# A decoder block with experts on one core: order of the last batch, two banks for late second layers, and one bias product for four tiles

## The chip, the core and the metric

The kernel runs on one core of a Trainium2 chip. TensorE (PE) multiplies, VectorE (DVE), ScalarE (ACT) and GpSimd (POOL) do the rest, and SyncE (SP) issues most of the transfers. Each engine works through its own instructions in order and waits on semaphores for the others. The metric is the device time of one execution in microseconds (us), lower is better.

## The reference

x is 4 batches of 1024 rows of 256 floats. Three blocks are added to it one after another, each of them on a layer norm of x:

```python
x = x + attention(layernorm(x))        # 16 heads of 16, scores / 4 - slope_h * |i - j|, softmax over 1024 keys
x = x + cross(layernorm(x), ctx)       # 77 context rows per batch, one head of 256
x = x + experts(layernorm(x))          # 8 experts, the best 2 per row

def experts(flat_x):                   # 4096 rows
    top_vals, top_idx = top_k(flat_x @ W_router + b_router, 2)
    w = softmax(top_vals)              # 0 for the other six
    for e in range(8):
        h = relu(flat_x @ W1[e] + b1[e])          # 256 -> 1024
        out += (h @ W2[e] + b2[e]) * w[:, e]      # 1024 -> 256
```

In the cross block the scores are `(x Wq + bq) (ctx Wk + bk)`; the kernel multiplies the query and key weights beforehand, so that a tile of rows is multiplied with `ctx_keys` (256 x 77) and the part that depends on the context row alone is the row `ctx_bias` (1 x 77).

## The kernel before

**One written order.** The function `plan` writes a list of steps. Every engine goes through this one list and issues the instructions that are its own, so the list fixes the order on PE, ACT, DVE, POOL and SP. `TAKES` holds a guessed duration for each kind of step; with it the planner keeps a clock of its own for each engine (`p.pe` is PE's), and puts a step off while the step that it reads isn't ready by these clocks (`until`).

**Attention.** 16 groups G of 4 heads, four groups to a batch. A group has 64 units. A unit is a `score` (PE, a 128x512 product for one head, line 1000, and near the diagonal a small second one, line 1003) and an `exp` (ACT, line 1233); after four units comes an `attend` (PE, 8 products, line 1014). The row maxima of the next group are worked out beside it: `max` (PE, line 1040, 1043) and `maxed` (DVE, line 1370). At the end of each half of a group come `av` (ACT), `av_turn` (PE, line 1022) and `on` (DVE).

**Side work.** Between the units the planner puts the steps of the batch whose attention is over (`complete`) and of the batch to come (`prepare`). How many is set by `PACE_DONE` and `PACE_NEXT`, one number per batch of the running attention: three of four units add that number to a share, capped at 12, and a step is issued while the share is above 0 and takes its price off (6 for a turn, 11 for half an `out`, 18 for half a `cross`, 16 for half a `cross_out`, 12 for half of `logits`, 4 for `rank`). `complete(b)` is the output projection (`out`, line 1092), a layer norm, the cross block (`cross`, lines 1104 and 1105; `cross_out`, lines 1123 and 1124), a layer norm, the routing (`logits`, line 1135, to `rows`, DVE line 1547), and 16 scatters of rows with their code, weights and number to the experts' regions in memory (`scatter`, POOL, line 1700), one after about every fourth unit: each waits for the `exp` in front of it in the order. The last batch is done in two halves of 512 rows, `FORE` as soon as the first half of the last group is there, and `AFT` after the attention.

**Experts.** 71 blocks of 128 rows. The table that says which expert and which rows each block takes is made in two parts, blocks 0 to 39 from the rows of three batches (`EARLY` is 40), the others once the last batch is routed. For a block n, SP issues two transfers (`load`): the first layer's weights `w1_now` (1 MB, line 967) and the rows `xi` (130 KB, line 971). For block 0 SP waits first for the table and for all scatters of the three batches. PE turns the rows (`xi_turn`, line 1191, bank 0), multiplies them with the first layer (`up`, two halves of 16 products, line 1203, banks 1 to 4), and with the second (`down`, 16 products, line 1221, the bank `AV_BANK`, number 7). ACT and DVE put bias and relu on the hidden rows (lines 1339 and 1615), DVE weighs the output (`yo`, line 1630), and POOL adds it to the result in memory (`added`, line 1714), each after the one before has landed. In the order, `up` of block n+1 and the turn of block n+2 stand ahead of `down` of block n. The two halves of the last batch are put between these steps one by one, from the first block on (`parts` and `next(work)` in `plan`).

**Banks.** PSUM has 8 banks of 512 floats per partition: 0 to 2 for scores, 3 and 4 for maxima, 5 and 6 (the ring "back") for all side steps, 7 for `attend` and, later, for `down`. A `down` waits until `yo` of the block before it has read bank 7.

Of the kernel before, what the change touches and what calls it, by code (L numbers as in the profile page):

```python
# [24 lines left out]
P = 128  # L25
NB, S, D = 4, 1024, 256
# [42 lines left out]
PACE_DONE = (4.0, 3.6, 3.6, 4.4)  # L69
# [147 lines left out]
def plan():  # L217
# [448 lines left out]
    parts = [done, complete(NB - 1, AFT)]  # L666
    while parts:
        parts = [part for part in parts if next(part, "end") != "end"]
        next(work)
# [17 lines left out]
def build(nc, t):  # L687
    p = plan()
    with ExitStack() as ctx:
# [136 lines left out]
        last_of = lambda tiles: tiles[1] - 1  # L826
        av_before = lambda G, ch: p.upto("av", *((G, 0) if ch else (G - 1, NCH - 1)))
# [11 lines left out]
        def _(e):  # L839
            def position_rows(i):  # L840

                for hh in range(HG):
                    e.dma_start(qa[i][SPECIAL:MAX_ROW, hh, :], qspec_dram).then_inc(sem["q_specials"], 16)

# [6 lines left out]
            for kind, *k in p.steps:  # L851
# [100 lines left out]
                elif kind == "load":  # L952
                    n, = k
                    if n == 0:
                        e.wait_ge(sem["table"], p.upto("table", 0, TABLE_PARTS - 1))
                        e.wait_ge(sem["scattered"], n_scatters(NB - 2))
                    elif n == 2:

                        e.wait_ge(sem["attend"], attend_of(LAST, NCH - 1, NT - 1))
                    elif n == EARLY:  # L960
                        e.wait_ge(sem["table"], p.upto("table", 1, TABLE_PARTS - 1))
                        e.wait_ge(sem["scattered"], n_scatters(NB - 1))
                        e.wait_ge(sem["idle_zeroed"], 16 * (NIDLE + 1 + NE))
                    if n >= NW:
                        e.wait_ge(sem["up"], p.upto("up", n - NW, 1))
                    of = e.value_load(expert_of[0:1, n:n + 1], min_val=0, max_val=NE - 1)
                    e.dma_start(w1_now[n % NW][:, :, :], t["w1"][bass.ds(of, 1)].rearrange("a (c p) f -> p (a c) f", p=P)).then_inc(sem[f"w1_in{n % NW}"], 16)
                    if n >= NX:
                        e.wait_ge(sem["added"], 16 * (n - NX + 1))
                    at = e.value_load(row_of[0:1, n:n + 1], min_val=0, max_val=NROW - P)  # L970
                    e.dma_start(xi[n % NX][:, :], rows_in[bass.ds(at, P), :]).then_inc(sem[f"slots_in{n % NX}"], 16)

        @block.tensor
        def _(e):
# [6 lines left out]
            for kind, *k in p.steps:  # L981
# [114 lines left out]
                elif kind == "cross":  # L1096
# [3 lines left out]
                    bank = side_bank(kind, *k, first=first)  # L1100
                    for q in (2 * part, 2 * part + 1):
                        tt, cols = 4 * four + q, slice(q * CTX, (q + 1) * CTX)
                        for c in range(DC):
                            e.matmul(ps[:, bank, cols], xT[:, c, tt * P:(tt + 1) * P], ctx_keys[:, b, c, :], start=(c == 0), stop=False)
                        m = e.matmul(ps[:, bank, cols], ones_row[:, :], ctx_bias[:, b, :], start=False, stop=True)
# [100 lines left out]
                elif kind == "down":  # L1206
                    n, = k
                    if n == 0:
                        e.wait_ge(sem["av"], p.counts["av"])
                        e.wait_ge(sem["weights_in"], 16 * NWEIGHTS)  # L1210
                    else:
                        e.wait_ge(sem["yo"], n)
# [3 lines left out]
                    for c in range(FC):  # L1216
# [4 lines left out]
                        m = e.matmul(ps[:, AV_BANK, 0:D], hidT[n % 2][:, c, :], w2[:, bass.ds(expert, 1), c, :].rearrange("p a f -> p (a f)"),  # L1221
# [133 lines left out]
        def _(e):  # L1355
# [10 lines left out]
            for kind, *k in p.steps:  # L1366
# [251 lines left out]
                elif kind == "yo":  # L1618
# [11 lines left out]
                    e.scalar_tensor_tensor(out=y[:, :], in0=ps[:, AV_BANK, 0:D], scalar=w[:, :], in1=bw[:, :],  # L1630
# [149 lines left out]
```

## Time and profile before

| | us |
|---|---|
| three runs | 1706.52, 1716.07, 1715.55 (median 1715.55) |
| profiled execution, its own time | 1717.18 |
| its span, first to last instruction | 1715.3 |
| mean granted clock of PE in it | 0.979 |
| PE busy | 1629.1 (95% of the span) |
| DVE, ACT, POOL busy | 1025.0, 788.5, 323.5 |

A busy PE is one with a product under way; products overlap, so the length of one says little, and the distance from one start to the next says what it costs. PEld is PE's weight load. "Idle before" is the time for which the engine stood still ahead of an instruction, with what ended it. The granted clock is a share of full speed: 1.00 is 2.4 GHz, 0.50 is 1.2 GHz. The attention runs until about 1124 us, the experts' blocks from about 1133 us to the end.

### The profile page before, as it was taken

What the parts mean: (1) busy time and instruction counts of PE and PEld (TensorE: products, weight loads), DVE (VectorE), ACT (ScalarE), POOL (GpSimd) and SP (SyncE); (2) the same over time, 40 slices, a digit from 0 to 9 for tenths busy, and PEclk for the clock granted to TensorE, in tenths of its full rate; (3) what the DMA queues carried; (4) which work ended last, traced back from release to release, by engine and by line L of the source; (5) the groups of instructions that cost most, each with busy time, mean ns of one, the idle gap of its engine ahead of it and who ended that gap; (6) DMA issues with size and microseconds to landing.
All of it is one profiled execution on the core that took longest, in us unless ns stands there. A gap on an engine that the chain in (4) does not pass through costs nothing.

```text
span 1715.3 us, 29817 instructions
## 1 busy us (share of the span) xinstructions
PE 1629.1 (95%) x10070; PEld 978.8 (57%) x10070; DVE 1025.0 (60%) x2366; ACT 788.5 (46%) x1635; POOL 323.5 (19%) x310
## 2 busy tenths in 40 slices
PE   4889999999999999999999999979999999999996
PEld 2433343344454444444443443359999889998986
DVE  4688777888777778777788774324344323333322
ACT  2136656667546666645666657732221212221221
POOL 6201120002100140210031100332144121222121
PEclk9799999999999999999999999989999999999999
DMA  6920441243140440342440621144566756666663
GB/s 171 181 64 26 77 78 18 25 65 42 39 77 26 78 79 11 34 72 66 65 68 25 139 84 66 60 154 135 154 192 182 206 164 177 185 167 174 184 159 73
DMA packets 92661, 173.31 MB, mean 101 GB/s; under 512 B 13235, under 2 KB 51123, under 8 KB 92384
## 3 DMA queue, kind: packets, MB, share of 16 engines
q1 hardware_dynamic: 75376, 143.69, 33.9%
q0 software_dynamic: 15744, 26.54, 7.4%
q10 hardware_dynamic: 1392, 1.18, 0.3%
q8 instruction: 83, 1.36, 0.3%
q14 instruction: 66, 0.54, 0.1%
HBM read 133.69 MB, written 37.29 MB: 100 GB/s over the span
## 4 chain that ended last, share of the span: by engine, by line
PE 88%; DVE 3%; ACT 3%; DMA 2%; issue 2%; POOL 1%; ACTq 0%; SPq 0%; DVEq 0%; POOLq 0%
PE ps L1014 15%; PE ps L1221 14%; PE ps L1203 14%; PE ps L1040 14%; PE ps L1000 13%; PE ps L1070 3%; DVE rmax L1370 2%; PE ps L1079 2%; ACT prob L1233 2%; PE ps L1123 2%; PE ps L1092 2%; PE ps L1061 2%; PE ps L1003 2%; PE ps L1043 2%; PE ps L1191 1%
## 5 line engine op out<-in xcount | busy, mean ns | idle before, releaser
L1370 DVE TENSOR_REDUCE rmax<-ps 128x1 f32<-128x512 f32 x1024 | 664.7, 686 | 212.3 <-PE ps L1040 106.8
L1233 ACT ACTIVATE prob<-ps 128x512 f32<-128x512 f32 x1024 | 562.6, 600 | 347.2 <-PE ps L1003 183.9
L1040 PE MATMUL ps<-stacked_k,stacked_q 112*128 112x512 bf16 x1024 | 394.5, 390 | 17.0 <-DVE rmax L1370 8.9
L1000 PE MATMUL ps<-stacked_q,stacked_k 115*128 115x512 bf16 x1024 | 361.0, 384 | 7.9 <-ACT prob L1233 5.4
L1014 PE MATMUL ps<-prob,values 128*32 128x512 f32 x2048 | 275.4, 610 | 7.0 <-ACT prob L1233 6.5
L1221 PE MATMUL ps<-w,hidT 128*128 x1136 | 260.3, 382 | 9.3 <-issue 7.4
L1203 PEld LDWEIGHTS ps<-xiT,w_now 128*128 128x128 f32 x2272 | 266.9, 193 | 3.7
L1203 PE MATMUL ps<-xiT,w_now 128*128 128x128 f32 x2272 | 268.6, 276 | 0.0
L1040 PEld LDWEIGHTS ps<-stacked_k,stacked_q 112*128 112x128 bf16 x1024 | 100.0, 98 | 294.0 <-DVE rmax L1370 204.1
L1339 ACT ACTIVATE hidT<-ps,b 128x128 f32<-128x128 f32 x284 | 81.3, 369 | 359.7 <-PE ps L1203 338.8
L1221 PEld LDWEIGHTS ps<-w,hidT 128*128 128x128 f32 x1136 | 210.1, 190 | 42.6 <-issue 16.4
L1615 DVE TENSOR_SCALAR hidT<-ps,b 128x128 f32<-128x128 f32 x284 | 80.1, 344 | 212.7 <-PE ps L1203 212.1
L1000 PEld LDWEIGHTS ps<-stacked_q,stacked_k 115*128 115x128 bf16 x1024 | 98.4, 99 | 164.1 <-ACT prob L1233 81.4
L1714 POOL DMA_INDIRECT out<-yo,xi x71 | 110.8, 1560 | 406.1 <-DVE yo L1630 393.2
L1003 PE MATMUL ps<-ramps,slopes 128*128 128x128 f16 x512 | 113.4, 222 | 0.0
L1043 PE MATMUL ps<-ramps,slopes 128*128 128x128 f16 x512 | 113.4, 221 | 0.0
L1630 DVE SCALAR_TENSOR_TENSOR yo<-ps,weight,bias 128x256 f32<-128x256 f32 x71 | 34.4, 484 | 128.1 <-PE ps L1221 128.1
L1648 POOL TENSOR_TENSOR rstd_of<-varp,minus_half 128x8 f32<-128x8 f32 (+1 forms) x14 | 20.8, 1487 | 388.3 <-DVE varp L1418 388.3
L1700 POOL DMA_INDIRECT expert_rows<-xn,slot x64 | 62.5, 977 | 160.7 <-ACT prob L1233 130.8
L1014 PEld LDWEIGHTS ps<-prob,values 128*32 128x32 f32 x2048 | 40.5, 108 | 81.3 <-issue 51.1
L1070 PE MATMUL ps<-xT_next,wqkv 128*128 128x512 f32 x128 | 68.6, 631 | 1.2 <-ACT xT_next L1259 0.9
L1043 PEld LDWEIGHTS ps<-ramps,slopes 128*128 128x128 f16 x512 | 50.7, 99 | 25.8 <-issue 9.4
(181 smaller groups left out, 1158.4 us busy)
## 6 DMA issues: line engine op xcount, KB each, us to landing
w_now<-in_w SPq DMA_DIRECT2D x71, 1024.0 KB
stacked_q<-parts_of_rows SPq DMA_DIRECT2D x90, 128.0 KB, 6.7
stacked_k<-parts_of_rows SPq DMA_DIRECT2D x90, 128.0 KB, 7.4
xi<-expert_rows SPq DMA_DIRECT2D x71, 130.0 KB
w<-in_w SPq DMA_DIRECT2D x8, 1024.0 KB, 9.3
parts_of_rows<-q_part SPq DMA_DIRECT2D x21, 256.0 KB, 7.9
parts_of_rows<-k_part SPq DMA_DIRECT2D x21, 256.0 KB, 7.9
xr<-in_x POOLq DMA_DIRECT2D x4, 1024.0 KB, 9.3
```

Source lines behind the costliest of these rows:

```text
L1000: m = e.matmul(ps[:, bank, :], ka[i][0:ROWS, hh, kt * P:(kt + 1) * P], qa[i][0:ROWS, hh, ch * BANK:(ch + 1) * BANK], start=True, stop=True)
L1003: m = e.matmul(ps[:, bank, (kt % 4) * P:(kt % 4 + 1) * P], slopes[:, g * HG + hh, :], ramps[:, kt % 2, :], start=False, stop=True, skip_gr ...
L1014: m = e.matmul(ps[CT * hh:CT * (hh + 1), AV_BANK, :], vt[b % 2][:, kt, c0:c0 + CT], prob[:, unit_of(G, ch, kt, hh) % NPROB, :], start=(kt ...
L1040: m = e.matmul(ps[:, bank, :], qa[i][0:MAX_ROW, hh, qt * P:(qt + 1) * P], ka[i][0:MAX_ROW, hh, kc * BANK:(kc + 1) * BANK], start=True, sto ...
L1043: m = e.matmul(ps[:, bank, (qt % 4) * P:(qt % 4 + 1) * P], slopes[:, g * HG + hh, :], ramps[:, 1 - qt % 2, :], start=False, stop=True, ski ...
L1070: m = e.matmul(ps[:, bank, :], wqkv[:, part, a * D + mo * P:a * D + (mo + 1) * P], xT_next[:, part, ch * BANK:(ch + 1) * BANK], start=firs ...
L1203: m = e.matmul(ps[:, 1 + 2 * (n % 2) + half, q * P:(q + 1) * P], w1_now[n % NW][:, c, f * P:(f + 1) * P], xiT[n % 2][:, c, :], start=(c == ...
L1221: m = e.matmul(ps[:, AV_BANK, 0:D], hidT[n % 2][:, c, :], w2[:, bass.ds(expert, 1), c, :].rearrange("p a f -> p (a f)"), start=(c == 0), s ...
L1233: e.activation(prob[:, u % NPROB, :], ps[:, u % NSCORE, :], ACT.Exp).then_inc(sem["exp"], 1)
L1339: m = e.activation(hidT[n % 2][:, q, :], ps[:, 1 + 2 * (n % 2), q * P:(q + 1) * P], ACT.Relu, bias=b1[:, bass.ds(expert, 1), q])
L1370: e.tensor_reduce(rmax[:, G % 2, hh * NT + qt, kc:kc + 1], ps[:, p.bank("max", *k), :], AX.X, ALU.max).then_inc(sem["maxed"], 1)
L1714: e.indirect_dma_start(t["out"], bass.IndirectOffsetOnAxis(ap=xi[n % NX][:, TOKEN:TOKEN + 1].bitcast(I32), axis=0), yo[n % NY][:, :], None ...
```

## The change

- `PACE_DONE` of the last batch is 5.4 and was 4.4.
- Between the attention and the blocks, the steps of both halves of the last batch are issued alone as long as the planner's clock of PE is less than 7.0 ahead of its last scatter; after that the blocks' steps go between them as before.
- SP issues the first layer's weights of blocks 0 and 1 between the wait for the table and the wait for the scatters; the rows follow after the scatters.
- From block 40 on, `down` and `yo` use banks 5 and 7 in turn, and `down` waits for the `yo` of two blocks before. Block 40 waits until the two last side steps have been read out of the ring.
- A `cross` of four tiles begins with one product of the bias row over 308 columns, in the place of one of 77 columns after each tile's products.

```diff
-PACE_DONE = (4.0, 3.6, 3.6, 4.4)
+PACE_DONE = (4.0, 3.6, 3.6, 5.4)
...
     work = blocks()
     parts = [done, complete(NB - 1, AFT)]
+    landed = p.made["scatter"] + 7.0
     while parts:
         parts = [part for part in parts if next(part, "end") != "end"]
-        next(work)
+        if p.pe >= landed:
+            next(work)
+        else:
+            p.at["pe"] += 0.1
...
+        down_bank = lambda n: NSCORE + NMAX if n >= EARLY and n % 2 == EARLY % 2 else AV_BANK
...
+            def first_layer(n):
+                of = e.value_load(expert_of[0:1, n:n + 1], min_val=0, max_val=NE - 1)
+                e.dma_start(w1_now[n % NW][:, :, :], t["w1"][bass.ds(of, 1)]...).then_inc(sem[f"w1_in{n % NW}"], 16)
...
                     if n == 0:
                         e.wait_ge(sem["table"], p.upto("table", 0, TABLE_PARTS - 1))
+                        first_layer(0)
+                        first_layer(1)
                         e.wait_ge(sem["scattered"], n_scatters(NB - 2))
...
-                    of = e.value_load(expert_of[0:1, n:n + 1], min_val=0, max_val=NE - 1)
-                    e.dma_start(w1_now[n % NW][:, :, :], t["w1"][bass.ds(of, 1)]...).then_inc(sem[f"w1_in{n % NW}"], 16)
+                    if n >= 2:
+                        first_layer(n)
...
                     bank = side_bank(kind, *k, first=first)
+                    if first:
+                        e.matmul(ps[:, bank, 0:4 * CTX], ones_row[:, :], ctx_bias[:, b, :].unsqueeze(1).broadcast_to([1, 4, CTX]), start=True, stop=True)
                     for q in (2 * part, 2 * part + 1):
                         tt, cols = 4 * four + q, slice(q * CTX, (q + 1) * CTX)
                         for c in range(DC):
-                            e.matmul(ps[:, bank, cols], xT[:, c, tt * P:(tt + 1) * P], ctx_keys[:, b, c, :], start=(c == 0), stop=False)
-                        m = e.matmul(ps[:, bank, cols], ones_row[:, :], ctx_bias[:, b, :], start=False, stop=True)
+                            m = e.matmul(ps[:, bank, cols], xT[:, c, tt * P:(tt + 1) * P], ctx_keys[:, b, c, :], start=False, stop=(c == DC - 1),
+                                         skip_group_check=True)
...
                     if n == 0:
                         e.wait_ge(sem["av"], p.counts["av"])
                         e.wait_ge(sem["weights_in"], 16 * NWEIGHTS)
+                    elif n == EARLY:
+                        for step in p.rings["back"][-NBACK:]:
+                            emptying = (EMPTIED[step[0]], *step[1:])
+                            e.wait_ge(sem[emptying[0]], p.upto(*emptying))
                     else:
-                        e.wait_ge(sem["yo"], n)
+                        e.wait_ge(sem["yo"], n if n < EARLY else n - 1)
...
-                        m = e.matmul(ps[:, AV_BANK, 0:D], hidT[n % 2][:, c, :], w2[...],
+                        m = e.matmul(ps[:, down_bank(n), 0:D], hidT[n % 2][:, c, :], w2[...],
...
-                    e.scalar_tensor_tensor(out=y[:, :], in0=ps[:, AV_BANK, 0:D], scalar=w[:, :], in1=bw[:, :],
+                    e.scalar_tensor_tensor(out=y[:, :], in0=ps[:, down_bank(n), 0:D], scalar=w[:, :], in1=bw[:, :],
```

## Rows read from the trace of the kernel before

**Rows 1.** Busy time by stretch: start:end length, engines (xinstructions), granted clock, DMA share, GB/s

```profile
200.00:1000.00 800.00, 790.58 (x4834) 346.93 (x4832) 624.57 (x1218) 499.88 (x938) 112.57 (x128) 0.99 0.30 54
885.00:1062.00 177.00, 172.41 (x1067) 75.30 (x1068) 129.53 (x248) 111.64 (x212) 22.12 (x26) 1.00 0.34 80
...
1072.70:1079.60 6.90, 6.21 (x27) 1.45 (x26) 2.76 (x14) 3.12 (x6) 0.00 (x0) 0.51 0.03 8
1079.60:1123.98 44.38, 40.38 (x255) 13.99 (x253) 15.14 (x68) 34.37 (x67) 18.32 (x20) 1.00 0.18 66
...
1127.40:1141.00 13.60, 4.94 (x22) 4.59 (x23) 0.00 (x0) 0.83 (x3) 0.90 (x2) 0.50 0.71 261
1141.00:1260.00 119.00, 119.00 (x810) 110.92 (x809) 48.89 (x182) 32.64 (x93) 27.37 (x23) 1.00 0.51 144
...
1475.00:1698.00 223.00, 218.83 (x1468) 201.62 (x1467) 69.71 (x239) 44.31 (x145) 45.01 (x29) 1.00 0.61 167
```

**Rows 2.** Timeline of PE from the attention's end: start, length, instructions, idle before

```profile
1124.76 0.66 PE L1022 MATMUL ps<-ident,av 128*128 128x128 f32 x4 [0.72 <-ACT av L1239]
1133.51 0.66 PE L1191 MATMUL ps<-ident,xi 128*128 128x128 f32 x2 [8.09 <-DMA xi<-expert_rows]
1136.72 0.66 PE L1191 MATMUL ps<-ident,xi 128*128 128x128 f32 x2 [2.56 <-DMA xi<-expert_rows]
1137.17 3.62 PE L1203 MATMUL ps<-xiT,w_now 128*128 128x128 f32 x16
1141.24 1.95 PE L1203 MATMUL ps<-xiT,w_now 128*128 128x128 f32 x16
1143.03 0.60 PE L1061 MATMUL ps<-ident,on 128*128 128x128 f32 x4
```

**Rows 3.** Timelines of POOL, DVE and SP: scatters, table's last instruction, first loads

```profile
1086.40 1.03 POOL L1700 DMA_INDIRECT expert_rows<-xn,slot  x1 [23.27 <-DVE xn L1547]
...
1124.54 0.98 POOL L1700 DMA_INDIRECT expert_rows<-xn,slot  x1 [0.31 <-issue]
1093.15 0.17 DVE L1601 SCALAR_TENSOR_TENSOR done_blocks<-end,nblocks 128x8 f32<-128x8 f32 x1
1128.07 0.41 SPq L967 DMA_DIRECT2D w_now<-in_w  x1
1129.27 0.35 SPq L971 DMA_DIRECT2D xi<-expert_rows  x1
...
1131.54 0.34 SPq L971 DMA_DIRECT2D xi<-expert_rows  x1
```

**Rows 4.** Timeline of PE in a cross step of batch 2, then the source view of line 1105

```profile
971.33 0.57 PE L1104 MATMUL ps<-ctx_keys,xT 128*128 128x77 f32 x4
...
972.20 0.67 PE L1104 MATMUL ps<-ctx_keys,xT 128*128 128x77 f32 x4
972.80 0.44 PE L1105 MATMUL ps<-ctx_bias,ones_row 1*128 1x77 f32 x2
973.17 0.39 PE L1040 MATMUL ps<-stacked_k,stacked_q 112*128 112x512 bf16 x1
L1105 PE MATMUL ps<-ctx_bias,ones_row x64: 270/318/329, 434.3 to 1205.1; 1*128 1x77 f32 x64
```

**Rows 5.** The chain of waits: an out step of 256 columns, start, us, what

```profile
1145.42 0.87 PE ps L1092 x4
```

**Rows 6.** Timelines of PE, DVE and POOL at the end

```profile
1700.23 3.72 PE L1221 MATMUL ps<-w,hidT 128*128 x16 [1.54 <-DVE yo L1630]
1699.55 1.55 POOL L1714 DMA_INDIRECT out<-yo,xi  x1 [5.47 <-DVE yo L1630]
1704.81 1.55 POOL L1714 DMA_INDIRECT out<-yo,xi  x1 [3.71 <-DVE yo L1630]
```

**Rows 7.** Waits view, 1300 to 1715 us: us in total, times, longest

```profile
PE ps L1221 <- DVE yo L1630: 1.5, 1, 1.5
```

**Rows 8.** DMA view, 1690 to 1716 us: GB/s in 40 slices of 0.65 us

```profile
GB/s 0 0 0 0 0 0 0 87 115 0 0 0 0 0 0 0 25 8 74 120 0 0 0 0 0 0 80 121 0 0 0 0 0 0 0 0 0 0 0 0
```

More of the change, by code:

```diff
@@ L843, in position_rows @@
                     e.dma_start(qa[i][SPECIAL:MAX_ROW, hh, :], qspec_dram).then_inc(sem["q_specials"], 16)
+            def first_layer(n):
+                of = e.value_load(expert_of[0:1, n:n + 1], min_val=0, max_val=NE - 1)
+                e.dma_start(w1_now[n % NW][:, :, :], t["w1"][bass.ds(of, 1)].rearrange("a (c p) f -> p (a c) f", p=P)).then_inc(sem[f"w1_in{n % NW}"], 16)
             for i in range(NT // 2):
@@ L965, in _ @@
                         e.wait_ge(sem["up"], p.upto("up", n - NW, 1))
-                    of = e.value_load(expert_of[0:1, n:n + 1], min_val=0, max_val=NE - 1)
-                    e.dma_start(w1_now[n % NW][:, :, :], t["w1"][bass.ds(of, 1)].rearrange("a (c p) f -> p (a c) f", p=P)).then_inc(sem[f"w1_in{n % NW}"], 16)
+                    if n >= 2:
+                        first_layer(n)
                     if n >= NX:
@@ L1220, in _ @@
                             e.wait_ge(sem["hid_aft"], n + 1)
-                        m = e.matmul(ps[:, AV_BANK, 0:D], hidT[n % 2][:, c, :], w2[:, bass.ds(expert, 1), c, :].rearrange("p a f -> p (a f)"),
+                        m = e.matmul(ps[:, down_bank(n), 0:D], hidT[n % 2][:, c, :], w2[:, bass.ds(expert, 1), c, :].rearrange("p a f -> p (a f)"),
                                      start=(c == 0), stop=(c == FC - 1))
```

## The prediction

> **What bounds the kernel now.** I read the page first (PE is busy for 95% of the span, the others for 60% and less), then the windows by stage, then the timeline where PE isn't full. Through most of the attention PE is under work for 790.6 of 800 us, and from 1141 to 1260 us for all of the 119 us [rows 1]. There only less work on PE shortens the time. Work that moves from one full stretch to another changes nothing.
>
> Two stretches are not full. The great one is the seam between attention and blocks: PE ends its last turn of the attention at 1125.42 (1124.76 + 0.66), then waits 8.09 us for the rows of block 0 and 2.56 us for those of block 1, and runs the first products at half speed [rows 2]. The granted clock over this stretch is 0.50, that is 1.2 GHz, after PE had stood still since 1125.4; it is at 2.4 GHz again from 1141.0 [rows 1]. The small one is the last group of the attention: 40.4 us busy of 44.4, with ACT at 34.4, so that ACT's exps set the pace for part of it. Just ahead of it lies another stretch of 6.9 us at 0.51 [rows 1].
>
> **The seam, in numbers.** Between 1125.42 and 1141.24 lie 15.82 us. At full speed the work done in them costs: `up` of 16 products 1.79 us (1141.24 to 1143.03 shows one), two turns of the rows and one side turn, 2 x 0.22 and 0.44, together 2.7. Lost: **13.1 us** [rows 2].
>
> What made PE wait is SP's order. The last scatter is issued at 1124.54 and SP's first load goes out at 1128.07: 1 MB of weights, and only 1.2 us later the 130 KB of rows of block 0, another 1 MB, and at 1131.54 the rows of block 1 [rows 3]. PE can turn the rows of block 0 4.2 us after their issue (1133.51) and those of block 1 5.2 us after theirs; they share the DMA engines with the weights. The table was complete at 1093.15, so the two weight transfers could have been issued 35 us earlier, over a stretch whose DMA share is 0.18 [rows 1, 3]; I cost them at nothing there, since no row of PE in the last group waits on a DMA.
>
> **Earlier weights.** Even with the scatters where they are, block 0's rows would be issued at about 1128.1, in the place of the weights, and block 1's 1.2 us later. Bounds for their way: no row shows one without 1 MB ahead, so at most the 4.2 us above, at least the 2.5 us from SP's wait after the last scatter's end (1125.52 to 1128.07), which also is a transfer alone. I take 3: block 1's rows are there at 1132.3 and not 1136.7.
>
> **Pace 5.4.** The steps of `complete` have a price list; for a whole batch it adds up to 388 (12 turns 72, 8 halves of `out` 88, 4 of `cross` 72, 8 of `cross_out` 128, `logits` 12, `rank` 4, `p_turn` 12). At 4.4 per call that is 88 calls, at 5.4 72; three calls to four units, so at most 21 of the batch's 256 units earlier. Dependencies that hold steps back (layer norms) eat part of it; I take 10 to 18 units. A scatter takes four units, 2.4 to 2.6 us (15 intervals from 1086.40 to 1124.54), so the routing and with it the last scatter come 7 to 14 us earlier, at 1111 to 1118, and the rows of both blocks are in place when PE ends the attention. It moves work from one part of the attention to an earlier one. What that costs lies between +3 us (the last group loses PE work that filled ACT's pace: its idle PE time of 4.0 us grows by as much again at the most) and -3.4 (the 6.9 us at half clock ahead of it go away, worth half of them) [rows 1]. I take 0.
>
> **Side steps ahead of the blocks.** They are held there only while the planner's PE clock is less than 7.0 ahead of its last scatter. If the scatters come 7 to 14 us earlier, that is over when the attention ends, and little or nothing is put in front; the steps then stay among the blocks, where PE is full, at no loss. If the scatters come late, turns and `out` of the second half (2 x 0.44 and 4 x 0.87 = 4.4 us) [rows 2, 5] fill the wait. Either way PE's work isn't lost.
>
> What of the seam stays: two turns with a copy by ACT between them, and the first side steps, whose attention output has to be divided by DVE first. I take 1.5 us of the 13.1 (between 0.7, one copy with its hops, and 4). **Gain 11.6 us.** SP's loads wait for nothing new; POOL, with its scatters done sooner, gets to the last batch's biases and its layer norm sooner.
>
> **Bias of four tiles at once.** In a cross step four products start at 971.33 and their bias follows, the next four start at 972.20 with theirs from 972.80, and the next instruction starts at 973.17: 1.84 us for two tiles. Eight plain products at 0.112 (1.79 / 16) would be 0.90. So a bias costs **0.47 us**, not the 0.22 of two plain products [rows 2, 4]. The source view counts 64 instructions of line 1105, two to a bias: 32 biases, 15.0 us. After the change there are 8, of 308 columns. A product of 256 columns costs 0.22 (0.87 for 4) [rows 5], so two of 308 cost 0.52; the rest of 0.47 that isn't columns (2 x 77 columns, 0.13) is 0.34 and stays. That makes 0.86 each, 6.9 us. The saving is 8.1 us: 2.0 in the last batch, all of it in full PE time, and 6.1 in the attention. There I count five sixths, since ACT or a maximum is sometimes what PE waits for. **Gain 7.1 us**, between 0 (what surrounds a one-row product comes again with every 77 columns) and 10.8 (it vanishes, and the product costs its columns alone).
>
> A smaller saving is possible. If a one-row product cost as little as a plain one, 0.22, and the 0.25 above it were only a pause that the neighbours make up, a step would save 4 x 0.22 - 0.52 = 0.36, and all eight 2.9 us. That is how a rule has it: the Trainium skill, TensorE: Matmul & The Clock Gate, sections "Back-to-back issue gap" and "LDWEIGHTS (loading the stationary operand)", gives a product the time of its columns and a weight load that of its columns too, whatever its rows. The starts in [rows 4], 0.47 us apart for what would be 0.22, don't agree with it for the old form; a one-row product of 308 columns stands in no row.
>
> **Second bank.** In all late blocks but one, `yo` is done long before `down` needs the bank: the wait is found once, 1.5 us [rows 7], ahead of the last `down`, which has no `up` in front of it [rows 6]. That wait goes. The 4.2 us that PE is idle between 1475 and 1698 [rows 1] have other causes and stay. The next in line is POOL's last addition, which waits for the one before it: issued 1699.55, its data move until about 1703 [rows 6, 8]; `yo` would come at 1703.0 in place of 1704.5. So nearly all of it arrives: **1.3 us** (0.5 to 1.5). Block 40 waits for two side steps read long before: nothing.
>
> **Sum.** 11.6 + 7.1 + 1.3 + 0 = 20.0 us. From the profiled execution's 1717.2: **1697 us**. That execution stands 1.6 above the median of the three, of which one is 9 us lower; I leave the forecast at 1697, which for the median (1715.6) would be 1.1% faster. About 1% is what a measurement of this kernel can tell from no change, and the bound is at 1698.4.
>
> **Rivals.**
> - *The seam closes only in part* (0.20). The planner's clock is no measure of real readiness. If the steps in front are many, PE goes through layer norm, turns and `out` in order, each behind ACT, DVE and POOL, while the rows already wait. For it: POOL adds the second half's biases only after its last scatter, and `out` is added after them. Against it: the guard ends them. Price 4 to 6 us, the half clock partly with it: 1702.
> - *The bias saves little* (0.12): 2.9 us in place of 7.1, by the mechanism above or because the attention doesn't pass on the 5.1 that I count there. For it: in the last group ACT sets part of the pace; against it: 790.6 of 800 us busy. 1701.
> - *Fewer stretches at half clock* (0.16). The dip ahead of the last group came after PE had run routing and turns of narrow output. With these steps moved beside maxima, and the one-row products gone, one or two such dips may go: 3.4 us each, 1691.
> - *Slower* (0.07). The denser side steps of the last batch stand in PE's order ahead of scores, and each waits for an ACT or DVE result that the planner believes ready. Today PE is idle for 4.6 us from 885 to 1062 and 4.0 in the last group. It decides at 20 more: some 30 turns and products pulled forward would have to wait 0.7 us each for the kernel to be no faster than 1717; at 1.3 us each it is 1736, over 1% slower.
>
> **Numbers.** Forecast 0.45, its own range 1693 to 1702. The range 1687 to 1707 takes in the second and third rival and most of the first, and leaves 2 in 10 out. Faster by over 1%: the better half of the forecast, the fewer dips, a little of the rest, 0.48. Within 1%: 0.46. Slower: 0.06.
>
> **What would show it.** In the changed kernel's timeline: the two weight loads near 1080 to 1093; the last scatter before 1120; `xi_turn` within 2 us of the last attention turn; granted clock 1.00 around it. Line 1105's successor with 16 instructions, starting before line 1104's, 0.86 us from its start to the first of theirs. No wait of `down` on `yo`. I am wrong if PE's wait at the seam is still over 4 us, if the one-row product takes less than 0.6 or over 1.1 us, or if PE's idle time from 885 us to the end of the attention has grown by more than 3.

## The result: 1692.2 us, 1.1% faster

| us | before | changed |
|---|---|---|
| median of the runs | 1713.55 (four: 1706.52 to 1716.07) | 1692.24 (four: 1691.19 to 1696.51) |
| profiled execution | 1717.18 | 1696.51 |
| mean granted clock in it | 0.979 | 0.982 |

The ratio is 0.9891, with a 95% interval of 0.9858 to 0.9924. From profile to profile the change took 20.7 us away where 20.0 were forecast. The profiled execution of the changed kernel is the slowest of its four. Of the 31 runs of the kernel before that stand beside the first experiments, one took 3698.3 us and is in none of the ratios.

**What the profile after shows.** The head of its page: span, busy time (share, instructions), then PE and its granted clock in 40 slices.

```profile
span 1694.7 us, 29721 instructions
PE 1617.0 (95%) x10022; PEld 968.4 (57%) x10022; DVE 1024.3 (60%) x2366; ACT 787.6 (46%) x1635; POOL 322.1 (19%) x310
PE   4889999999999999999999999989999999999997
...
PEclk9789999999999999999999999999999999999999
```

PE has 12.1 us less of work at the same share of the span. The same stretches as in [rows 1], in the same columns: the middle of the attention, the half-clock stretch ahead of its last group, that group, the seam, and a new half-clock stretch.

```profile
200.00:1000.00 800.00, 791.16 (x4874) 344.45 (x4873) 632.17 (x1231) 506.20 (x950) 112.35 (x128) 1.00 0.30 54
1055.40:1063.90 8.50, 8.50 (x47) 3.84 (x45) 3.15 (x15) 3.92 (x7) 0.00 (x0) 0.60 0.00 0
1063.90:1109.60 45.70, 42.15 (x269) 14.58 (x262) 15.13 (x68) 35.63 (x69) 17.45 (x20) 1.00 0.32 111
1113.16:1123.53 10.37, 7.72 (x48) 6.47 (x49) 3.68 (x9) 4.40 (x9) 4.40 (x7) 1.00 0.40 142
1312.90:1316.30 3.40, 3.40 (x10) 2.68 (x9) 0.00 (x0) 0.00 (x0) 0.00 (x0) 0.51 0.91 290
```

The seam, from the end of the last attention turn to the first side turn after 16 products of `up`, is 10.4 us long. PE works in 7.7 of them, and the granted clock is 1.00. Before, the seam of the prediction's working was 15.8 us long, and [rows 1] had 4.9 us busy in 13.6 at 0.50. PE's timeline over it, with the columns of [rows 2]:

```profile
1112.50 0.66 PE L1036 MATMUL ps<-ident,av 128*128 128x128 f32 x4 [0.72 <-ACT av L1261]
1113.97 1.09 PE L1075 MATMUL ps<-ident,on 128*128 128x128 f32 x8 [0.81 <-DVE on L1417]
1116.34 2.86 PE L1106 MATMUL ps<-wo,xT 128*128 128x256 f32 x12 [1.28 <-ACT xT L1281]
1119.28 0.63 PE L1075 MATMUL ps<-ident,xn 128*128 128x128 f32 x4
1119.75 1.03 PE L1106 MATMUL ps<-wo,xT 128*128 128x256 f32 x4
1120.61 0.38 PE L1208 MATMUL ps<-ident,xi 128*128 128x128 f32 x2
1121.47 0.44 PE L1208 MATMUL ps<-ident,xi 128*128 128x128 f32 x2 [0.47 <-ACT xiT L1347]
1121.74 1.95 PE L1220 MATMUL ps<-xiT,w_now 128*128 128x128 f32 x16
1123.53 0.60 PE L1075 MATMUL ps<-ident,xn 128*128 128x128 f32 x4
```

No wait on a DMA is left, and side steps stand in front of the first `xi_turn`: two turns, four quarters of `out` and a turn of the layer norm. SP's queue and POOL's scatters, as in [rows 3]:

```profile
1079.46 1.59 SPq L854 DMA_DIRECT2D w_now<-in_w  x2
1114.18 1.46 SPq L985 DMA_DIRECT2D xi<-expert_rows  x2
```

```profile
1071.47 1.03 POOL L1722 DMA_INDIRECT expert_rows<-xn,slot  x1 [23.93 <-DVE xn L1569]
...
1110.95 1.02 POOL L1722 DMA_INDIRECT expert_rows<-xn,slot  x1 [0.50 <-ACT prob L1255]
```

The weights left 35 us ahead of the rows. The scatters, though, are only a little earlier against the work beside them: from the first one to the end of the attention PE needs 41.7 us (1071.47 to 1113.16), where it was 39.0 (1086.40 to 1125.42). The cross step, in the place of [rows 4], timeline and source view (shortest, median, longest, first and last start):

```profile
950.83 0.78 PE L1117 MATMUL ps<-ctx_bias,ones_row 1*128 1x308 f32 x2
951.54 1.12 PE L1121 MATMUL ps<-ctx_keys,xT 128*128 128x77 f32 x8
...
L1117 PE MATMUL ps<-ctx_bias,ones_row x16: 416/469/522, 435.4 to 1158.9; 1*128 1x308 f32 x16
```

It takes 0.71 us from its start to the first product of the keys. The product ahead of it starts at 950.68 and, by the other pairs beside it, takes 0.06, so that PE turns to the bias at 950.74: about 0.80 us with this entry of 0.09. At the end, in the place of [rows 6], DVE and POOL:

```profile
1682.12 0.48 DVE L1652 SCALAR_TENSOR_TENSOR yo<-ps,weight,bias 128x256 f32<-128x256 f32 x1 [1.55 <-PE ps L1243]
1679.42 1.55 POOL L1736 DMA_INDIRECT out<-yo,xi  x1 [5.47 <-DVE yo L1652]
1684.03 1.55 POOL L1736 DMA_INDIRECT out<-yo,xi  x1 [3.06 <-DMA out<-yo,xi]
```

`down` no longer waits. The last addition now does, for the one before it to land: 1.4 us from the end of `yo` (1682.60) to its issue.

### The profile page after: what moved, and what is told of

Its sections match the earlier page's. It is cut to its first block, busy times and chain, and to the rows that moved or that the text cites. A ratio compares the mean times of both kernels' runs of the same rounds, so it can differ in the third digit from the quotient of the medians.

```text
span 1694.7 us, 29721 instructions
## 1 busy us (share of the span) xinstructions
PE 1617.0 (95%) x10022; PEld 968.4 (57%) x10022; DVE 1024.3 (60%) x2366; ACT 787.6 (46%) x1635; POOL 322.1 (19%) x310
## 4 chain that ended last, share of the span: by engine, by line
PE 86%; DMA 5%; DVE 3%; ACT 3%; issue 2%; POOL 1%; SPq 0%; ACTq 0%; DVEq 0%; POOLq 0%
PE ps L1028 15%; PE ps L1054 14%; PE ps L1243 13%; PE ps L1014 13%; PE ps L1220 12%; DMA out<-yo,xi 3%; PE ps L1084 3%; DVE rmax L1392 2%; ACT prob L1255 2%; PE ps L1093 2%; PE ps L1106 2%; PE ps L1140 2%; PE ps L1075 2%; PE ps L1057 2%; PE ps L1017 2%
## 5 line engine op out<-in xcount | busy, mean ns | idle before, releaser
L1054 PE MATMUL ps<-stacked_k,stacked_q 112*128 112x512 bf16 x1024 | 395.2, 390 | 15.7 <-DMA stacked_k<-parts_of_rows 7.4
L1243 PEld LDWEIGHTS ps<-w,hidT 128*128 128x128 f32 x1136 | 211.4, 191 | 40.7 <-issue 14.3
```

What stands on the lines that cost most here:

```text
L1054: m = e.matmul(ps[:, bank, :], qa[i][0:MAX_ROW, hh, qt * P:(qt + 1) * P], ka[i][0:MAX_ROW, hh, kc * BANK:(kc + 1) * BANK], start=True, sto ...
L1243: m = e.matmul(ps[:, down_bank(n), 0:D], hidT[n % 2][:, c, :], w2[:, bass.ds(expert, 1), c, :].rearrange("p a f -> p (a f)"), start=(c == ...
```

## The experiments

The parts of the change overlap in the time, so they were tried alone and taken out one by one. "Median" is that of the runs of the kernel named; each ratio is against the kernel before, run beside it (1708.94 us in the first set of four kernels, 1707.02 in the second, 1707.49 in the third; each set ran on a chip of its own). A figure in brackets is the 95% interval.

### Parts alone on the kernel before

**The bias alone.**

```diff
...
+                    if first:
+                        e.matmul(ps[:, bank, 0:4 * CTX], ones_row[:, :], ctx_bias[:, b, :].unsqueeze(1).broadcast_to([1, 4, CTX]), start=True, stop=True)
...
-                        m = e.matmul(ps[:, bank, cols], ones_row[:, :], ctx_bias[:, b, :], start=False, stop=True)
```

> The kernel before with the bias product over 308 columns alone; all else as it was. Theory A (a one-row product costs a fixed pause of about 0.34 us beside its columns): a cross step of four tiles takes 1.0 us less, eight of them 8.1 us; the exps of the attention come 2.2 us earlier after each of the three cross blocks, so 1706 to 1709 us against 1714. Theory B (the change also takes away the half-clock windows near 571 and 731 us, because the one-row products were what PE did before them): the attention ends 11 to 12 us earlier, 1701 to 1704 us, and no window at 0.50 between 120 and 1040 us. Rival C (the one-row product pays its pause with every 77 columns): same time as before.

Measured: 1700.32 us, ratio 0.9947 (0.9931 to 0.9964), that is 9.1 us (6.2 to 11.8). This lies between theory A (5 to 8 us) and theory B (10 to 13). Theory B's sign is there, no stretch at half clock between 120 and 1040 us in this trace, but its ground holds for one of the two stretches at most: the one near 571 us stands in four traces of kernels with a merged bias. Counted from the first exp, the last exp of the attention starts at 1002.6 us, before at 1012.7. The 10.1 us between them: each of the three cross blocks in the attention gives 2.2 to 2.4 (at exp 384, for one, 380.7 for 382.9), so the saving arrives in full; 3.2 are a stretch at half clock near 571 us that comes and goes from one execution to the next; 1.6 are one near 730 us; and 1.7 are lost again ahead of the last group, where half clock lasts 10.2 us for 6.8. The one near 730, worth 1.6 to 3.2, stands in all five traces with the old bias and in none of nine with a merged one. Windows of a second run of the kernel before, then of this kernel:

```profile
727.00:733.80 6.80, 6.80 (x44) 4.19 (x42) 4.78 (x10) 2.83 (x6) 0.47 (x1) 1.00 0.43 164
733.80:737.20 3.40, 3.40 (x8) 1.28 (x8) 2.25 (x4) 0.60 (x1) 0.00 (x0) 0.50 0.37 143
```

```profile
728.00:736.00 8.00, 8.00 (x49) 2.81 (x51) 6.99 (x13) 5.04 (x10) 1.76 (x2) 1.00 0.07 28
```

PE counts as busy for the whole 6.8 us ahead of the fall, here and in the four other traces, so it hadn't stood still. That the one-row products bring it on is what five traces against nine suggest; how they would is not shown.

**The weights alone.**

```diff
                         e.wait_ge(sem["table"], p.upto("table", 0, TABLE_PARTS - 1))
+                        first_layer(0)
+                        first_layer(1)
                         e.wait_ge(sem["scattered"], n_scatters(NB - 2))
...
```

> The kernel before with the weights of blocks 0 and 1 sent before SP's wait for the scatters; order of steps, pace, banks and bias as before. Theory A (the two earliest transfers of weights held the rows back): rows of block 1 are there at about 1131 to 1132 in place of 1136.7, PE still has nothing to do from 1125.4 and falls to half clock; 4 to 6 us less, 1708 to 1710. Rival (the rows' own way is what takes long): under 2 us.

Measured: 1704.35 us, 0.9971 (0.9948 to 0.9995), 4.9 us (0.9 to 8.9), as theory A has it. PE's timeline at the seam:

```profile
1130.83 0.66 PE L1197 MATMUL ps<-ident,xi 128*128 128x128 f32 x2 [4.49 <-DMA xi<-expert_rows]
1132.02 0.66 PE L1197 MATMUL ps<-ident,xi 128*128 128x128 f32 x2 [0.53 <-ACT xiT L1331]
```

The rows of both blocks are there together, and the waits of 8.09 and 2.56 us [rows 2] are 4.49 and none. The rows' way, for which no row before stood free of weights, takes 2.2 us here, from SP's issue at 1128.66 to PE's first turn (the DMA list has a median of 2.1 over all blocks), less than the 3 that I took.

**The steps alone**, and **both** (steps in front and early weights).

```diff
+    landed = p.made["scatter"] + 7.0
...
-        next(work)
+        if p.pe >= landed:
+            next(work)
+        else:
+            p.at["pe"] += 0.1
```

> The kernel before with the last batch's first steps alone in front of the blocks while the planner's clock is less than 7.0 ahead of the last scatter; weights are sent late, as before. Theory A: 5 to 6 us of turns and out products run between 1126 and 1136; the rows come as late as before, at 1136.7, but PE's clock stays or comes back to full; 5 to 7 us less, 1707 to 1709. Rival (PE walks a chain of ACT and DVE waits and loses there what it gains): within 2 us of before.

> The kernel before with both: weights early and steps in front; pace 4.4, banks and bias as before. Theory A: the steps fill the time until the rows are there, PE idles 3 to 4 us in all between attention and blocks, 9.5 to 11 us less than before, 1703 to 1704. Rival (what closed the seam in the changed kernel is the earlier routing by pace 5.4): 5 us less at most.

Measured: the steps alone 1714.77 us, 1.0035 (1.0014 to 1.0056), which is **slower** by 6 us (2 to 10), and neither theory has that. Both 1704.81, 0.9987 (0.9958 to 1.0015), no gain that can be told from none, where 9.5 to 11 us were expected. What takes back the steps' gain stands in the windows of the steps kernel (first and second line) and of the kernel before, run again (the line by itself):

```profile
1127.20:1139.70 12.50, 7.75 (x46) 5.87 (x44) 4.17 (x14) 4.89 (x10) 7.04 (x10) 1.00 0.70 265
1139.70:1153.40 13.70, 13.70 (x59) 12.83 (x59) 2.22 (x8) 2.09 (x6) 0.00 (x0) 0.50 0.08 31
```

```profile
1129.70:1143.40 13.70, 5.46 (x25) 5.12 (x26) 0.00 (x0) 1.34 (x5) 0.92 (x2) 0.50 0.69 259
```

Both kernels get 13.7 us of half clock near the seam. Before, it lies over a PE that has nothing to do for 8.2 of them. With the steps in front it comes later, over the first blocks' products, where PE is busy for all of it. At half speed 13.7 us of busy PE cost 6.8, and 5.46 cost 2.7: the 4.1 between them take back most of what the steps filled in. They had filled in 5.2 us by the durations of the prediction (two turns of `on` 0.88, four quarters of `out` 3.5, two turns of layer norm 0.88); I had counted 4.4. The waits alone gave no sign of that. It explains that next to nothing is gained, but not the loss of 2 us or more beyond it: the profiled execution of the steps kernel, 1710.87 us, was itself shorter than both of the kernel before (1717.18 and 1716.23), so its trace need not hold the cause, which stays open. In the kernel with both, 3.4 us of half clock fall in the same place, and the seam itself lies open for another reason:

```profile
1133.64 0.63 PE L1071 MATMUL ps<-ident,xn 128*128 128x128 f32 x4
1134.11 1.03 PE L1102 MATMUL ps<-wo,xT 128*128 128x256 f32 x4
1135.92 0.66 PE L1071 MATMUL ps<-ident,xn 128*128 128x128 f32 x4 [0.78 <-DVE xr L1476]
1136.41 0.38 PE L1201 MATMUL ps<-ident,xi 128*128 128x128 f32 x2
1137.54 0.44 PE L1201 MATMUL ps<-ident,xi 128*128 128x128 f32 x2 [0.74 <-ACT xiT L1335]
```

Its rows were issued at 1129.82 and so were there at about 1132, and PE waits for none of them. It does two turns of layer norm and a quarter of `out` first, the last of them behind DVE. That is the rival "closes only in part", in this kernel.

### Parts taken out of the changed kernel

**The changed kernel again, and without its guard** (`next(work)` in each turn of the loop, as before, so that no steps are held in front of the blocks).

> The changed kernel once more, to be compared with the three others of this call on the same chip. Ratio to the kernel before 0.988 to 0.991; no window at half clock between 120 and 1040 us; attention to last turn 1003 us after the first exp minus nothing else, as in its first profile (1001.6).

> The changed kernel without the steps in front of the blocks; pace, early weights, banks and bias as changed. Theory A (the steps in front give little by themselves, since the rows come 3 to 4 us after the attention's end): PE idles 3.5 to 4.5 us at the seam in one piece and loses 1 to 2 us more than with the steps; within 2 us of the changed kernel. Rival (the steps are what keeps the clock up): a window at half clock over the first blocks, 4 to 6 us slower.

**With the pace of before.**

```diff
-PACE_DONE = (4.0, 3.6, 3.6, 5.4)
+PACE_DONE = (4.0, 3.6, 3.6, 4.4)
```

> The changed kernel with pace 4.4 in the last batch; the rest as changed. Theory A (pace 5.4 moves the routing by about 4 units, 2 to 3 us, and no more, and the steps in front then run past the landing of the rows into a window at half clock): 3 to 6 us slower, the attention 2 to 4 of it. Rival (the pace only reorders work on a full PE): within 1.5 us.

Measured:

| kernel | median, us | ratio | last attention turn ends | block 1's rows turned | first exp to exp 960 |
|---|---|---|---|---|---|
| changed, again | 1688.79 | 0.9877 (0.9834 to 0.9920) | 1110.8 | 1120.6 | 954.1 |
| without guard | 1690.66 | 0.9893 (0.9843 to 0.9942) | 1112.4 | 1116.8 | 954.6 |
| old pace | 1694.61 | 0.9909 (0.9872 to 0.9946) | 1117.5 | 1127.5 | 957.8 |

The changed kernel again is as fast as it was, but two of its signs missed: its ratio is a little under the range, and 3.4 us of half clock stand at 570.9 us, where none was expected. The guard's worth is 1.9 us between medians, within the intervals: theory A's time. But a stretch at half clock over the first blocks is there, as the rival has it. Without the guard PE waits for block 0's rows and then meets 6.8 us of half clock over full work:

```profile
1115.64 0.66 PE L1204 MATMUL ps<-ident,xi 128*128 128x128 f32 x2 [3.30 <-DMA xi<-expert_rows]
1117.27 3.62 PE L1216 MATMUL ps<-xiT,w_now 128*128 128x128 f32 x16
```

The pace is worth 5.8 us between medians, though these intervals overlap too. Ahead of exp 960 the old pace is 2.3 to 3.7 us later (957.8, for 955.5, 954.1 and 955.3 in three executions of the changed kernel). Of the 2.3, 1.4 are the stretch near 571 us, which the first of the three executions doesn't have; that leaves 0.9 to 3.7. 1.0 of it lies between exp 768 and 896 in each of the three. The rest goes with the stretch at half clock ahead of the last group: 3.4 us at the old pace, and 6.8, none and 3.4 in the three. The seam takes as long up to block 1's rows (10.0 us, for 9.8), but with one turn more in it, and 3.4 us of half clock follow over full work from 1130.1, as the expectation has it: by the table at the end of the next section it loses 6.3 us, for 3.4 to 5.0.

### Earlier scatters

The changed kernel's seam still holds work in front of rows that come late, since the last scatter ends 1.2 us ahead of the attention. Two ways to bring it forward: in all three batches a scatter after about every second unit (first), or in the third batch alone one after every third unit (second).

```diff
-                while p.pe < p.made.get("scatter", 0.0) + 0.7:
+                while p.pe < p.made.get("scatter", 0.0) - 0.6:
```

```diff
-                while p.pe < p.made.get("scatter", 0.0) + 0.7:
+                if b == NB - 2:
+                    yield
+                    yield
+                while b < NB - 2 and p.pe < p.made.get("scatter", 0.0) + 0.7:
```

> The changed kernel with scatters one after every second unit (the planner waits until 0.6 before the last one's end and no longer 0.7 after it), so that they end some 25 units before the attention does; the guard is then met from the start and no step stands in front of the blocks. Theory A (the seam is made by the rows' lateness alone): block 0 is turned within 1.5 us of the last attention turn, PE loses 1 to 1.5 us in place of 3.3, no half clock; 1 to 3 us faster than the changed kernel. Rival (scatters at twice the rate hold up the exps or other transfers): the last group of the attention takes 2 us or more longer.

> The changed kernel with the 16 scatters of batch 2 one after every third unit (batches 0 and 1 as before); they end 7 units before the attention does in place of 1 to 2, and by the planner's clock the guard lets one side step stand in front of the blocks. Theory A (rows in place when the attention ends close the seam; what held up the attention with scatters after every second unit was a burst of them, one per 1.3 us): block 1 is turned 1 to 3 us after the last attention turn in place of 8 to 10, with 4.4 us less side work in front, last group of the attention within 1 us of the changed kernel; 1 to 3 us faster. Rival (closer scatters cost the attention as much as they give): the last group 2 to 4 us longer, no gain.

Measured: the first 1697.65 us, 0.9928 (0.9905 to 0.9952), which is slower than the changed kernel by 8.9 us between medians of one set, as the rival has it. The second 1685.99, 0.9866 (0.9842 to 0.9890), beside the changed kernel once more at 1689.71, 0.9894 (0.9870 to 0.9917), whose expectation was:

> The changed kernel, beside the version with scatters after every third unit, on the same chip. Ratio to the kernel before 0.987 to 0.990.

The first closes the seam wholly and loses 12 us in the attention (last exp at 1010.3, not 998.5). Its timelines of POOL and ACT where the scatters are thick:

```profile
1080.04 0.97 POOL L1722 DMA_INDIRECT expert_rows<-xn,slot  x1 [0.30 <-issue]
...
1083.86 1.03 POOL L1722 DMA_INDIRECT expert_rows<-xn,slot  x1 [0.31 <-issue]
```

```profile
1085.92 2.06 ACT L1255 ACTIVATE prob<-ps 128x512 f32<-128x512 f32 x4 [3.04 <-remote]
```

Scatters follow each other every 1.27 us (1080.04 to 1083.86), and then ACT stands still for 3.04 us with nothing in the trace that released it; 6.8 us of half clock follow. It happens in the first batch's scatters too:

```profile
599.53 2.06 ACT L1255 ACTIVATE prob<-ps 128x512 f32<-128x512 f32 x4 [2.43 <-remote]
```

Here 3.4 us of half clock follow. The second batch's scatters, as close, show no such wait, but from exp 640 to 768 there are still 2.5 us more. In none of the other 13 traces does an `exp` wait for more than 0.25 us for something that the trace doesn't show ("remote"). Of the 11.8 us, 4.6 lie between exp 384 and 512, 2.5 between 640 and 768 and 5.7 behind 960; 1.2 are won back between 896 and 960. In the second kernel, PE's timeline:

```profile
1109.79 0.65 PE L1039 MATMUL ps<-ident,av 128*128 128x128 f32 x4 [0.72 <-ACT av L1264]
1111.25 0.66 PE L1078 MATMUL ps<-ident,on 128*128 128x128 f32 x4 [0.81 <-DVE on L1420]
1111.74 0.38 PE L1211 MATMUL ps<-ident,xi 128*128 128x128 f32 x2
1112.93 0.44 PE L1211 MATMUL ps<-ident,xi 128*128 128x128 f32 x2 [0.80 <-ACT xiT L1350]
```

The last scatter starts at 1103.69, the rows are issued at 1106.85, and the first block's rows are turned 1.3 us after the last turn of the attention, at full clock. It is the fastest version, 3.7 us under the changed kernel between medians; the run ranges (1682.04 to 1687.69, 1687.94 to 1692.73) are apart, the intervals of the two ratios overlap.

**What each kernel loses at the seam.** The working of the prediction can be done for every kernel: the time from the end of the attention's last turn to the first product of `down`, less what PE's work in it costs at full speed. The kernel before, with a line that [rows 2] leaves out, and the changed one:

```profile
1140.59 0.82 PE L1061 MATMUL ps<-ident,on 128*128 128x128 f32 x4
1148.99 3.62 PE L1221 MATMUL ps<-w,hidT 128*128 x16
```

```profile
1132.24 3.62 PE L1243 MATMUL ps<-w,hidT 128*128 x16
```

For the kernel before that is 23.6 us for three turns of rows (0.66), 64 products of `up` (7.16), two turns of `on` (0.88) and two quarters of `out` (1.74). The kernels with a guard do two more quarters (1.74), two turns of layer norm (0.88) and, but for the one with the third batch's scatters earlier, a cross step of four tiles (3.68, merged 2.59) in the same place.

| kernel | time, us | work | lost | half clock in it |
|---|---|---|---|---|
| before | 23.6 | 10.4 | 13.1 | 13.7 |
| bias alone | 23.3 | 10.4 | 12.8 | 13.7 |
| weights alone | 17.4 | 10.4 | 6.9 | 6.8 |
| steps alone | 28.8 | 16.7 | 12.1 | 13.7 |
| both | 23.2 | 16.7 | 6.4 | 3.4 |
| changed (three executions) | 19.1, 20.6, 19.1 | 15.7 | 3.4, 5.0, 3.4 | 0, 3.4, 0 |
| without guard | 17.4 | 10.4 | 6.9 | 6.8 |
| old pace | 22.0 | 15.7 | 6.3 | 3.4 |
| third batch's scatters earlier | 14.9 | 13.1 | 1.8 | 0 |
| all scatters closer | 10.9 | 10.4 | 0.5 | 0 |

Each row but that of the changed kernel is one trace. The early weights are the great part of what the seam gained (6.2 us), the steps in front alone give 1.0, and only guard and new pace together bring 6.9 or 6.3 down to 3.4 to 5.0. The timed runs pass on less of it: the kernel with both gained 6.7 at the seam by its trace, and 2.2 us (-2.6 to 7.2) in its runs; where the rest went is not shown.

### What a one-row product costs, and what an execution does

```diff
-                    if first:
-                        e.matmul(ps[:, bank, 0:4 * CTX], ones_row[:, :], ctx_bias[:, b, :].unsqueeze(1).broadcast_to([1, 4, CTX]), start=True, stop=True)
+                    e.matmul(ps[:, bank, 2 * part * CTX:(2 * part + 2) * CTX], ones_row[:, :], ctx_bias[:, b, :].unsqueeze(1).broadcast_to([1, 2, CTX]), start=first, stop=True, skip_group_check=True)
```

> The changed kernel with one bias product for two tiles (154 columns), in front of each half of a cross step. Theory A (a pause of about 0.34 us for every one-row product, whatever its columns): 0.26 + 0.34 = 0.60 us each from its start to the first ctx_keys product, 1.2 us a step in place of 0.86 predicted and some 0.71 read after the change. Rival (the pause grows with the columns): 0.35 to 0.45 us each, the same per step as one product over 308 columns.

> The kernel before once more, for its windows at half clock. Theory A (the window near 730 us belongs to the old form of the bias, the one near 571 us comes and goes): a window begins between 727 and 733 us. Rival (both are chance): none there.

Measured, one run each: 1699.87 us for two tiles to a bias, 1716.23 for the kernel before. PE's timeline in the former:

```profile
709.91 0.52 PE L1115 MATMUL ps<-ctx_bias,ones_row 1*128 1x154 f32 x2
710.36 1.12 PE L1119 MATMUL ps<-ctx_keys,xT 128*128 128x77 f32 x8
```

From one start to the next that is 0.45 us for 2 x 154 columns and 0.71 for 2 x 308. So 154 more columns, twice, cost 0.26, what the columns of a plain product cost; about 0.20 is fixed and some 0.09 lies in its entry. The 0.34 that I kept as fixed is near 0.29. The number is the rival's, but not its ground: the fixed part is the same for 154 and 308 columns.

In its two traces the kernel before has its exps at the same places within 0.1 us as counted from the first one, and the second has the stretch near 730 us too (733.8, with a first exp that comes 2.3 us later). The first exp starts between 109.7 and 113.5 us after the span's start in all these traces. The blocks differ more from execution to execution: from the end of the attention to the last `down` the changed kernel took 565.2, 558.5 and 556.8 us in three executions, the one before 574.8 and 571.6. The waits of PEld, the weight load, ahead of `down`, 1124 to 1697 us, in the changed kernel's profiled execution and in the third one:

```profile
PEld ps L1243 <- issue: 14.3, 27, 1.0
```

```profile
PEld ps L1243 <- issue: 7.7, 16, 0.7
```

Between them lie 6.6 us, of a difference of 8.4 between these two executions: time in which the weight load waits for nothing that the profile shows. Differences of a few us between single traces in the blocks are therefore not read here; the timed ratios decide.

## Why the prediction was right, and where it was not

**The bound.** Right: less PE work came through one to one (8.6 us by the traces, 9.1 timed), and the seam was the other place. Of the signs, the weight loads (1079.46), the 16 bias instructions, the clock at the seam and `down` without a wait came, and PE's idle time from 885 us to the end of the attention fell from 10.0 to 7.7 us. The turn of the rows within 2 us did not; the last scatter came at 1110.95, before 1120, because the whole attention ended 12 us earlier.

**Seam, 11.6 us of 13.1.** Between 1113.16 and 1123.53 PE does 7.05 us of work by the durations of the working (two turns of `on` 0.88, 16 products of `out` 3.5, one layer-norm turn 0.44, the rows' turns 0.44, `up` 1.79). Lost: 3.3 us, so the gain is 9.8. The half clock, which stood before over a seam in which PE had nothing to do, is gone in this execution; in another 3.4 us of it stand there, and 5.0 us are lost. The step "the scatters come 7 to 14 us earlier, and little or nothing is put in front" failed. Against the attention's end the first scatter moved 2.7 us, some four units, where I took 10 to 18 of at most 21 (by the 2.54 us of a scatter, which takes four units, these are 6 to 11 us and not 7 to 14); what held the steps back, no run tells. So 4.8 us of steps were put in front, and the rows were turned not within 2 us of the last attention turn, but 7.5 us after it (1113.16 to 1120.61). The guard, which I counted as without effect, is what fills the seam at pace 5.4; timed, that is worth 1.9 us, within the noise. The kernel with the third batch's scatters earlier holds one turn in front of the blocks and is faster.

**Pace, 0.** Taken too low. With the old pace the attention takes 0.9 to 3.7 us more, without the chance of the stretch near 571; I had 3.4 as one end, for the half-clock stretch ahead of the last group. That stretch is still 6.8 us long in the profiled execution (8.5 at 0.60 on the mean), 3.4 in another and absent in the third, so only about 1 us is sure. The timed 5.8 us hold 1.3 to 2.9 of the seam besides (6.3 lost there with the old pace, 5.0 to 3.4 with the new), a gain that stands above under the seam.

**Bias, 7.1.** Taken too low. The product itself is 0.80 us for the forecast 0.86, so a step saves 1.08 and eight save 8.6. "Five sixths in the attention" failed: each of its cross blocks gives 2.2 to 2.4 us, all of it. The stretch at half clock near 730 us, 3.4 to 6.8 us long, comes on top. A rule would have had it otherwise: the Trainium skill, TensorE: Matmul & The Clock Gate, section "Back-to-back issue gap", gives an isolated product the time of its columns and little more, and says that in a stream this counts too little at small column numbers. By the 0.22 of one 256-column product [rows 5], columns alone would be 0.26 and 0.52 here; the starts are 0.45 and 0.71 apart. The time by columns holds for the difference and not for the product.

**Second bank, 1.3.** The wait went, and 0.5 arrives: from the start of the last but one `down` to the end it is 19.8 us for 20.2. I had the addition before landing at about 3.4 us from its issue. The next one is issued only 4.6 us after it (1679.42 to 1684.03); from issue to landing the DMA view has a median of 3.9 between 1600 and 1696 us.

**The sum.** That 20.0 came so near to 20.7 is in part luck, for it hides errors of both signs: seam -1.8, bank -0.8, the bias with the stretch at 730 +3, the pace +1 or more. In these two traces the stretch at 571 adds 3.2 by chance, the first exp starts 1.9 later, and the rest was given back in the blocks, 1.7 of it in the half-clock stretch at 1313 us.

**The rivals.** "Closes only in part" (1702) happened in small at pace 5.4: PE goes through four quarters of `out` and a turn of layer norm while the rows, issued at 1114.18, are there (from about 1116.4 on, by the 2.2 us of their way), but it costs 1.8 us and not 4 to 6. In the kernel with both parts at pace 4.4 it costs more: 6.4 us stay lost. "The bias saves little" is refuted. "Fewer stretches at half clock" (1691) happened for one stretch, and the median of 1692.2 lies nearer to it than to the forecast, which was made for the slower profiled execution. "Slower" is not the changed kernel: PE's idle time in the last group is 3.55 us of 45.7, for 4.0 of 44.4. But parts of it in other company do lose, and in their traces stand two things that I had not named: half clock over full work (the steps alone), and scatters too thick.

**Open.** Whether the one-row products cause the stretch at 730, what stopped ACT behind the thick scatters, and what makes the kernel with the steps alone slower than the one before, and why the runs of the kernel with both show so little of what its seam gained. No kernel with the second bank alone was run, so its 0.5 us rests on the two traces.

## What to carry to other kernels

Cover for a late transfer is worth what the engine really does in it: before you fill a gap, look at where the clock is low, since a stretch at half speed costs little over an idle engine (2.7 us for 13.7 here) and half its length over a full one (6.8). Send the large transfer that needs no late result ahead of the wait, and check that what is put in the gap isn't itself a chain through three engines. A bias product of one row paid about 0.3 us here beside its columns, so gather such rows into one.

## What was not expected of the hardware

- Half clock came near 730 us with PE under products for all of the 6.8 us before it, in 5 of 5 traces with one-row products of 77 columns and in 0 of 9 with 154 or 308 columns.
- Scatters 1.27 us apart were followed by 3.04 us of ACT without a visible releaser, and in another batch by 2.43; a third batch had none. With one after every third unit, 1.9 us apart for the most part, there was none.
- The weight load's unexplained waits ahead of `down` add up to 7.7 us in one execution and 14.3 in another of the same kernel.
- The first exp starts anywhere between 109.7 and 113.5 us, for work that doesn't differ.
